# AdaLN stencil and two-layer FFN with folded outer products: the first batch in 384 and 128 tokens, row scalars as the second load, layer 2 weight tiles moved in the queues

## The reference, cut to what matters

```
y   = zX*lap_x(x) + zY*lap_y(x) + zR*x*(1-x)              # per batch, (1024, 512), reflecting edges
lt  = y[:, 1:17];  even = lt[:, ::2];  odd = lt[:, 1::2]
m1  = even[:, :4, :, None] * odd[:, :4, None, :]  -> (B, 2048, 512)
m2  = even[:, 4:, :, None] * odd[:, 4:, None, :]  -> (B, 512, 2048)
h   = gelu(y @ W1.T + scale * y @ m1.T + b1)              # exact gelu
out = x + h @ W2.T + scale * h @ m2.T + b2
```

## Time and profile before

| | |
|---|---|
| median of three runs | 1374.31 us |
| lowest, highest | 1370.9, 1374.43 us |
| the profiled execution | 1370.56 us, its span 1368.8 us |
| mean granted TensorE clock | 0.993 |
| TensorE busy | 1346.0 us, 98% |
| VectorE, ScalarE, GpSimd busy | 1071.4 (78%), 806.0 (59%), 419.4 us (31%) |
| DMA | 262.56 MB, mean 192 GB/s |

### The profile page before, as it was taken

One profiled execution on the slowest core, in us unless ns is written; L12 is line 12 of the kernel. 1 busy time (PEld: TensorE's weight loads), 2 busy tenths in 40 slices (PEclk: granted clock), 3 DMA queues, 4 the chain that ended last, 5 costly groups with the idle time before them and its releaser, 6 DMA issues.

```text
span 1368.8 us, 17057 instructions
## 1 busy us (share of the span) xinstructions
PE 1346.0 (98%) x5834; PEld 1095.8 (80%) x5834; DVE 1071.4 (78%) x1681; ACT 806.0 (59%) x1406; POOL 419.4 (31%) x403
## 2 busy tenths in 40 slices
PE   8799999999999999999999999999999999999999
PEld 3588787888878888788887888878887888888887
DVE  6899889967899578995799857997689967675343
ACT  3675557745666556664566645675557654576432
POOL 5354134421345113441144502443033530123100
PEclk9899999999999999999999999999999999999999
DMA  5687687865778577776768757777487866777461
GB/s 141 166 207 228 198 214 206 209 186 209 182 211 210 161 223 181 212 217 170 220 165 228 195 180 231 177 214 196 163 219 209 214 177 201 170 204 192 131 200 54
DMA packets 134438, 262.56 MB, mean 192 GB/s; under 512 B 15312, under 2 KB 23632, under 8 KB 134352
## 3 DMA queue, kind: packets, MB, share of 16 engines
q1 hardware_dynamic: 116328, 209.95, 47.7%
q0 software_dynamic: 17664, 50.34, 21.9%
q10 hardware_dynamic: 360, 1.19, 0.3%
HBM read 194.06 MB, written 67.37 MB: 191 GB/s over the span
## 4 chain that ended last, share of the span: by engine, by line
PE 82%; DVE 11%; ACT 3%; issue 1%; DVEq 0%
PE po L444 15%; PE po L445 15%; PE po L446 15%; PE ph L427 13%; PE ph L429 12%; PE ph L431 12%; DVE W2s L412 4%; DVE yl L298 1%; DVE xr L520 1%; DVE W2l L419 1%; ACT R L354 1%; DVE W1l L370 1%; DVE gl L462 1%; DVE W1l L373 1%; DVE y L288 1%
## 5 line engine op out<-in xcount | busy, mean ns | idle before, releaser
L444 PE MATMUL po<-W2h,gh 128*128 128x512 f32 x1024 | 398.5, 389 | 0.7 <-DVE gl L462 0.7
L445 PE MATMUL po<-W2l,gh 128*128 128x512 f32 x1024 | 398.4, 389 | 0.0
L446 PE MATMUL po<-W2h,gl 128*128 128x512 f32 x1024 | 398.4, 389 | 0.0
L427 PE MATMUL ph<-yh,W1h 128*128 128x512 f32 x896 | 353.0, 394 | 13.4 <-ACT UVs L473 7.1
L429 PE MATMUL ph<-yl,W1h 128*128 128x512 f32 x896 | 350.4, 391 | 0.0
L431 PE MATMUL ph<-yh,W1l 128*128 128x512 f32 x896 | 350.4, 391 | 0.0
L462 DVE TENSOR_TENSOR gl<-ph,gh 128x512 fp32r<-128x512 f32 x256 | 175.6, 686 | 190.1 <-ACT gh L460 189.9
L457 ACT ACTIVATE ph<-ph,b1t 128x512 f32<-128x512 f32 x256 | 167.1, 653 | 167.3 <-DVE ph L502 62.4
L412 DVE SCALAR_TENSOR_TENSOR W2s<-EB,SC,W2s 128x128 f32<-128x128 f32 x512 | 246.4, 537 | 1.2 <-DMA W2s<-in_w_dram 1.2
L460 ACT ACTIVATE gh<-ph 128x512 fp32r<-128x512 f32 x256 | 152.5, 596 | 131.9 <-PE po L446 129.4
L444 PEld LDWEIGHTS po<-W2h,gh 128*128 128x128 f32 x1024 | 192.2, 188 | 41.3 <-DVE gl L462 1.1
(11 more groups left out here) (85 smaller groups left out, 1230.6 us busy)
## 6 DMA issues: line engine op xcount, KB each, us to landing
R<-in_w_dram POOLq DMA_DIRECT2D x64, 512.0 KB, 7.5
W2s<-in_w_dram SPq DMA_DIRECT2D x128, 256.0 KB, 4.3
uv_scratch<-UVs SPq DMA_DIRECT2D x128, 256.0 KB, 3.8
UVs<-uv_scratch SPq DMA_DIRECT2D x128, 256.0 KB, 4.1
X<-in_xT_dram SPq DMA_DIRECT2D x56, 390.0 KB, 3.9
td_scratch<-Ts SPq DMA_DIRECT2D x64, 256.0 KB, 4.9
xr<-in_x_dram SPq DMA_DIRECT2D x16, 1024.0 KB, 6.1
xr<-in_b_dram POOLq DMA_DIRECT2D x16, 1024.0 KB, 10.7
```

Source lines behind the costliest of these rows:

```text
L427: e.matmul(bank[:, :], W1h[:, f, blk, wc], yh[:, s, c, :], start=first and c == 0, stop=False, skip_group_check=not first)
L444: e.matmul(po[t][:, :], gh[:, late, st], W2h[:, k, :], start=first, stop=False)
L445: e.matmul(po[t][:, :], gh[:, late, st], W2l[:, k, :], start=False, stop=False)
L446: mm = e.matmul(po[t][:, :], gl[:, late, st], W2h[:, k, :], start=False, stop=last)
```

## The change

- *Row scalars as second load.* `scale` becomes a fourth column of `z`; the scalars of the 64 rows (`zn`) are one DMA where there were two. SP's order becomes z, zn, x0, x1, xs, x3, x6, x4, x5, x7; x1 moves from ScalarE's queue to SP, and x2 on ScalarE's behind the first activation.
- *Sums of quarters in 384 and 128 tokens.* Tiles 6 and 7 of the first batch change roles (6 is now made early by VectorE, 7 last by TensorE). operands(0) runs on tokens 0 to 383 and 384 to 511; the low part of S1's first piece goes behind that of S2's second.
- *Row factors of blocks 2 and 3 of the first batch* come in one broadcast of 512 columns into slot 3 of `UVs`, where each had its own EB1; block 2's scalings, its GpSimd DMA and its waits move ahead, block 3's behind block 1's start. For block 1 the GpSimd sums and the parts move behind.
- *Layer 2 parts behind copies.* In the first batch the folds and parts of W2 tiles 0 and 1 go behind the copies of products 6 and 5; tiles 2 to 7 follow half a block later.
- *Layer 2 tiles of other batches.* In all other batches the even tile of a block moves from T+12.5, T+22.5, T+27 (folds, high, low) to T+0.5, T+13, T+17, the odd one from T+35.5, T+42, T+47.5 to T+22, T+33, T+37; tiles 0 to 3 come one block of half 1 earlier. Their loads move along. Slots 5 and 6 move from T+13 and T+67 to T+15.9 and T+69.9. GpSimd's sums for the next batch's stencil get larger numbers.

```diff
-        k_zn = d_zn.dma(sp, us(0.1), [(zn[:, 0:3], bass.AP(z.tensor, 0, [[3, 8], [0, 8], [1, 3]])),
-                                      (zn[:, 5:6], bass.AP(scale.tensor, 0, [[0, 64], [1, 1]]))])
+        k_zn = d_zn.dma(sp, us(0.1), [(zn[:, 0:4], bass.AP(z.tensor, 0, [[4, 8], [0, 8], [1, 4]]))])
...
-            k = d_xs.dma(sp, when - 80 if b else us(1.4),
+            k = d_xs.dma(sp, when - 80 if b else us(0.4),
...
-                load = us((0.05, 0.5, 0.4, 0.6, 1.6, 1.7, 1.8, 1.5)[n])
-                adds = us((0, 0, 8, 10.7, 0, 0, 17, 13.4)[n])
+                load = us((0.2, 0.25, 2.1, 0.6, 1.6, 1.7, 1.5, 1.8)[n])
+                adds = us((0, 0, 8, 10.7, 0, 0, 13.4, 17)[n])
...
-                    load, adds, mul, fin = T - 7, (T + 25, T + 30), T + 38.5, (T + 43, T + 47, T + 51)
+                    load, adds, mul, fin = T - 7, (T + 32, T + 37.5), T + 38.5, (T + 43, T + 47, T + 51)
...
-            if b == 0 and n not in (3, 7):
-                bank = (po[0], po[1], po[2], None, po[3], ph[1], ph[3])[n]
+            if b == 0 and n not in (3, 6):
+                bank = (po[0], po[1], po[2], None, po[3], ph[1], None, ph[3])[n]
...
-                cut = slice(0, 512) if b else slice(256 * q, 256 * q + 256)
+                cut = slice(0, 512) if b else slice(384, 512) if q else slice(0, 384)
...
-                hi = [ytile.at(b, n) for n in (range(4, 8) if b or q else (4, 5))]
+                hi = [ytile.at(b, n) for n in (range(4, 8) if b or q else range(4, 7))]
...
-                parts(b, w[4], 2, S1, p5.at(b - 1, 7), m1, cut=cut)
+                parts(b, w[4], 2, S1, p5.at(b - 1, 7), m1, cut=cut, lag=5 if b or q else 11)
...
-            parts(b, T + 13 if b else T + 67, 5, A21, p7.at(b - 1, 7), addS.at(b, "S3"))
-            parts(b, T + 67 if b else T + 121, 6, A22, p4.at(b - 1, 7), *[ytile.at(b, n) for n in range(4, 8)])
+            parts(b, T + 15.9 if b else T + 69.9, 5, A21, p7.at(b - 1, 7), addS.at(b, "S3"))
+            parts(b, T + 69.9 if b else T + 123.9, 6, A22, p4.at(b - 1, 7), *[ytile.at(b, n) for n in range(4, 8)])
...
-            ahead = (-134, -110, -100) if b and i == 1 else (-116, -90, -80) if i == 1 else \
+            ahead = (-134, -110, -100) if b and i == 1 else (-116, -90, -80) if i == 1 else (-180, -138, -129) if b == 0 and i == 2 else (-180, -92, -84) if b == 0 and i == 3 else \
...
-            w = [T + a for a in (*ahead, -50, -43, -39, -30, -45, -36, -28, -21)] if b or i else \
+            w = [T + a for a in (*ahead, *((-36, -29, -25, -36, -30, -20, -17, -10) if (b, i) == (0, 1) else
+                                     (-50, -43, -39, -30, -45, -36, -28, -21)))] if b or i else \
...
+            if b == 0 and i in (2, 3):
+                if i == 2:
+                    k_e01[0] = d_uv[3].dma(sp, w[0], [(UVs[:, 3, 256 * a:256 * a + 256], EP[1:2, 256 * a:256 * a + 256].broadcast_to(
+                        [128, 256])) for a in range(2)], k_ep)
+                k, even = k_e01[0], UVs[:, 3, 256 * i - 512:256 * i - 256]
...
-            free = [loT.at(b, i - 2), tops.at(b, i - 2)] if i > 1 else \
+            free = [None if b == 0 and i == 2 else loT.at(b, i - 2), tops.at(b, i - 2)] if i > 1 else \
...
-                T = t0(b - 1, 1, 4 + n)
+                T = t0(b - 1, 1, 3 + n)
                 return T + 13, T + 21.2, T + 28
             T = t0(b, 0, (n - 4 if b else n) // 2)
-            return (T + 35.5, T + 42, T + 47.5) if n % 2 else (T + 12.5, T + 22.5, T + 27)
+            if b == 0 and n < 2:
+                return (T + 30, T + 43, T + 48) if n else (T + 16, T + 36.5, T + 41)
+            if b == 0 and 2 <= n < 7:
+                n, T = n + 1, t0(b, 0, (n + 1) // 2)
+            elif b == 0 and n == 7:
+                return T + 48, T + 56, T + 59
+            return (T + 22, T + 33, T + 37) if n % 2 else (T + 0.5, T + 13, T + 17)
...
-                k_e2[b, jk] = d_e2.dma(sp, when - 28, [(
+                k_e2[b, jk] = d_e2.dma(sp, when - 26, [(
...
-            kd = d_w[s].dma(sp, when - (41 if n % 2 else 38), [(W2s[:, s, :], w2[k])], w2lo.at(*past2))
+            kd = d_w[s].dma(sp, when - (38 if n % 2 else 36), [(W2s[:, s, :], w2[k])], w2lo.at(*past2))
```

More of the change, by code:

```diff
@@ L3, with adaln_ffn_kernel @@
 from contextlib import ExitStack
-def adaln_ffn_kernel(nc: bass.Bass, xT, xs, x, z, w1, b1, w2, b2, scale, out):
+def adaln_ffn_kernel(nc: bass.Bass, xT, xs, x, z, w1, b1, w2, b2, out):
     f32 = mybir.dt.float32
@@ L58, in adaln_ffn_kernel @@
         junk = sb("junk", [128, 1])
-        zt = sb("zt", [128, B, 3])
+        zt = sb("zt", [128, B, 4])
         zc = sb("zc", [128, 2, B])
@@ L191, in coefficients @@
             return dve.put(when + 0.3, lambda e: e.tensor_tensor(zz[4], zz[4], zz[2], ALU.add), a)
-        m_zn = coefficients(us(4.4), [zn[:, i:i + 1] for i in range(5)], k_zn)
+        m_zn = coefficients(us(4.4), [zn[:, i:i + 1] for i in (0, 1, 2, 4, 5)], k_zn)
         m_zc = coefficients(us(3), [zt[:, :, 0], zt[:, :, 1], zt[:, :, 2], zc[:, 0, :], zc[:, 1, :]], k_z)
         m_dg = pool.put(us(4), diagonal(3, zc[:, 1, 0:1]), m_zc)
-        m_nw = act.put(us(6.0), lambda e: e.activation(nW, N[:, 1, :], ACT.Identity, bias=zn[:, 4:5],
-                                                       scale=zn[:, 3:4]), k_N, m_zn)
+        m_nw = act.put(us(6.0), lambda e: e.activation(nW, N[:, 1, :], ACT.Identity, bias=zn[:, 5:6],
+                                                       scale=zn[:, 4:5]), k_N, m_zn)
         m_na = pool.put(us(6.0), lambda e: e.tensor_tensor(nA, N[:, 0, :], N[:, 2, :], ALU.add), k_N)
@@ L259, in stencil @@
             mid, up, down, left, right = [x_[:, r:r + 4, c:c + 128] for r, c in ((1, 1), (0, 1), (2, 1), (1, 0), (1, 2))]
-            kx = d_x[s].dma(act if b == 0 and n in (1, 2) else sp, load, [(x_.rearrange("p r s -> p (r s)"), xT[b, n])], *free_x)
+            kx = d_x[s].dma(act if b == 0 and n == 2 else sp, load, [(x_.rearrange("p r s -> p (r s)"), xT[b, n])], *free_x)
             by_pool = b > 0 or n in (2, 3, 6, 7)
@@ L275, in products @@
                     return emit
-                at = us((5, 9.6, 14.9, 0, 17.8, 22.3, 26.8)[n])
+                at = us((5, 9.6, 14.9, 0, 17.8, 22.3, 0, 26.8)[n])
                 if n == 0:
@@ L293, in adaln_ffn_kernel, with parts @@
         S1 = xr[:, 0:2, :]
-        def parts(b, when, slot, src, free, *after, cut=slice(0, 512)):
+        def parts(b, when, slot, src, free, *after, cut=slice(0, 512), lag=5):
             yh, yl, s = (yh0, yl0, slot) if slot < 5 else (yh1, yl1, slot - 5)
             a = act.put(when, lambda e: e.activation(yh[:, s, :, cut], src[:, :, cut], ACT.Copy), free, *after)
-            opd[b, slot] = dve.put(when + 5, lambda e: e.tensor_tensor(
+            opd[b, slot] = dve.put(when + lag, lambda e: e.tensor_tensor(
                 yl[:, s, :, cut], src[:, :, cut], yh[:, s, :, cut].bitcast(f32), ALU.subtract), a)
```

20 lines of the change are left out of this document (11 added, 9 removed).

## The result

1411.70 us, median of four runs (1410.50 to 1413.48), against 1372.77 us for the kernel before (four runs, 1370.90 to 1374.43): the ratio is 1.0285, 95% interval 1.0264 to 1.0306. The change makes the kernel slower by 39 us. The forecast was 1382 us within 1363 to 1391: right in direction and in the wait it named, far short in size. The measured time lies above the range.

A forecast was written before the change was run, and what follows sets the result against it. TensorE, busy 98% of the span, was taken to bound the kernel. 1370.56 - 1.2 (start) + 10.8 (six batches) = 1380.2, plus 1.9 towards the runs' median, gave 1382 us; range 1363 to 1391.

The forecast's parts named there:

- What bounds the kernel: TensorE, busy 98%: at most 22.8 us to gain, of which two small pauses a batch, six times, cost 8.5 us.
- The start: First block, before the regular batches: loads, 384/128 sums, row factors and later W2 tiles gain 1.2 us, bounds 0 and -5.5.
- 60% of 1.4 us: First block: product 3 starts at 50.2, not 51.58; its half-clock matmuls let through 60% of that.
- Block 1: Batches 1 to 6: held folds delay product 6's copy to 395.8, so product 5 waits up to 3.6 us, 3.2 taken.
- the holds of block 0: Block 0 of batch 2: GpSimd holds VectorE instructions 2.3 us instead of 1.9, so L288 starts at 388.2; called the weakest step.
- Net of the 1.4 that goes: +1.8 a batch, six batches, +10.8 us: Batches 1 to 6: product 5's wait of 3.2 us less the old small pauses; bounds 0 and +13 us.
- Blocks 2 to 5 ... No further wait, with nothing to spare: VectorE's work of 8.65 us plus holds of 3.5 fills 12.15 of each block's 12.24 us, adding no wait.
- Batch 0 ... none: First batch: one fold less by block 2 and no evictions in block 0, so no further wait.
- Rival 4: EB2's single buffer loads late, 3.5 us against 4.0 of room: at most 0.5 us in two blocks a batch; no chance given.
- Rival 3: TensorE's clock falls in the new pause, losing 2 to 4 us in three to six batches: 1388 to 1400 us; chance 0.1.
- GpSimd's additions "move in their numbers alone": Batches from 2 on: GpSimd's adds get new planned times but keep their order; no size given.
- Rivals 1 and 2: First: gaps close, nothing replaces them, 1363.6 us, chance 0.27. Second: a wash, wait 1.5 to 2 us, 1370 to 1377, chance 0.23.

The follow-up runs named there:

- the cut additions: Start-only kernel with five GpSimd additions (three row-factor, two stencil in block 1) cut to 8 columns in batches 1 to 6: 1361.07 us, 0.9921.
- start-only kernel: Changed kernel with batches 1 to 7, and batch 0's layer 2 tiles 2 to 15 and slots 5 and 6, planned as before: 1369.80 us, 0.9992.
- the holds of block 1 cut away: Changed kernel with five GpSimd additions (three row-factor, two stencil in block 1) cut to 8 columns in batches 1 to 6: 1385.56 us, 1.0106.
- the kernel with the filled pause: Changed kernel with 30 matmuls of zeros ahead of product 5 of block 1 in batches 1 to 6: 1409.01 us, 1.0288.
- with both taken away: Changed tiles in batch 0 alone, two EB2 reloads left out, batch 0's GpSimd additions cut to 8 columns: 1367.34 us; start-only kernel with those additions cut: 1365.62 us.
- the kernel with the stencil additions back: Changed kernel with GpSimd's stencil additions planned at T + 25 and T + 30 again, not T + 32 and T + 37.5: 1409.31 us, 1.0275.
- the last of the four tries: Start-only kernel with block 1's two stencil additions at T + 39 and T + 44 in batches 1 to 6, their readers later: 1368.61 us, 0.9982.

## Why the prediction was right or wrong

- *What bounds the kernel*: right. The 8.5 us of the small pauses, and GpSimd's hold as their cause, are measured by the cut additions (1369.80 to 1361.07 us).
- *The start*, -1.2 with bounds 0 and -5.5: inside its bounds, -0.8 (0.9992, 0.9983 to 1.0001), which is also not to be told from nothing. The working inside is off: product 6 comes 0.94 us sooner and not 0.2 later, product 3 2.33 sooner and not 1.4, and in the start-only kernel the gain is lost in block 2. Nor does -1.2 follow from its own terms, as 60% of 1.4 us is 0.8; no run shows the 60%. The first pause is still 5.00 us, as said.
- *Block 1*: right in its marks. Counted from when product 5 could have started (409.06 here, 392.26 before), the row factors' addition starts at 386.8 in the time of before (387.0 forecast), the last fold ends at 393.6 (393.6) and the copy of product 6 at 395.7 (395.8). Product 5 waits 3.45 to 3.52 us (3.2 taken, 3.6 the long end), six times. The step that it called its weakest, the holds of block 0, came out otherwise: the row factors' addition held L286 (2.22 us), the step before the one named, and the folds began at 390.2 and not 389.6. It made no difference, because they end with GpSimd's last addition.
- **"Net of the 1.4 that goes: +1.8 a batch, six batches, +10.8 us"** is one of the two terms that failed: 5.25 a batch, 31.5 us. The wait itself cost 3.6, with the refilling behind it, and not 3.2; the 1.4 did go. The other 3.0 are the half clock (about 2.1) and waits behind block 2 (0.9). The subtraction assumed that a wait of 3.2 ends the matter. But by "Blocks 2 to 5 ... No further wait, with nothing to spare" VectorE was at 12.15 of 12.24 us, and what comes on top of the wait is VectorE's lateness, which has no block to be made up in. It showed mostly as half clock in the changed kernel and as waits in blocks 2 to 5 in the kernel with the filled pause, at the same time in all. With the holds of block 1 cut away, 24 to 26 us of it went, 9 of which the old order gains by that cut as well; that VectorE's lateness is the cause is shown by the filled pause for the clock's part, and argued from its busy time for the rest.
- **"Batch 0 ... none"** is the other: 12 us in the profile; with the rest undone 7 to 8.5. Of these, 3 to 4 are EB2's reload, the rest held folds (with both taken away, 1367.34 us against 1365.62). Rival 4 had put EB2 at "at most 0.5 us in two blocks", from 3.5 us of load against 4.0 of room; in batch 0 tile 7 sits right ahead of tile 8 (T + 48, next T + 0.5) and the load took 4.8 us: no room at all. That plan's own numbers showed it, and I had worked it out for the other batches only. There the rival was right: in batches 1 to 5 of the changed kernel VectorE waits for EB2 twice a batch, for 0.2 to 0.5 us.
- *Rival 3*, the clock: it fell in all six of the new pauses, and in five of the same six in the kernel with the stencil additions back, so the chance of 0.1 was far too low. The Trainium skill, in "TensorE: Matmul & The Clock Gate", section "HAM oscillation — how this bites in real kernels", cited there, speaks of pauses that cost the clock each time; the granted clock agrees in 11 of these 12. The rival's price of 2 to 4 us a batch isn't borne out: about 2 us on the spot, and some 0.3 by the next batch, as another engine was behind.
- *GpSimd's additions "move in their numbers alone"*: right. In the order of batch 2 nothing changed, and in the last of the four tries a due time 14 units later still moved nothing.
- Rivals 1 and 2: not seen. Both needed VectorE further ahead in block 1, and it came behind GpSimd.

What stays open: the half of the loss in batches 1 to 6 that does not hang on the holds of block 1, and whether some other order frees both tiles' folds at once. The extra loss in batch 0 of the full change over its parts (12 against 7 us) looks like the spread of executions: the kernel with the filled pause, whose batch 0 is the changed kernel's, stands 7.7 us behind the kernel before at the start of batch 1, the changed kernel 11.5.

## To carry to other kernels

When an engine has 1% of its time to spare over several blocks, price its lateness as what comes out at the end of those blocks, not as the first wait that it makes: the first wait, the clock and the later waits pay the same debt. When a run leaves work out to test a cause, leave the same work out of the old kernel too, or what both gain is counted as the change's. Work through the first and the last iteration with their own numbers; a single buffer that just has room in the steady state has none where two users stand side by side. A copy in an in-order queue is as late as the latest thing queued ahead of it, so put what the critical engine needs ahead of what only the next step needs.
